# A graph kernel of hops, attention, messages and convolutions on one core: edge features stored by the counting and loaded per step, more PSUM banks per step, and fixed codes compared per edge

## The reference, cut to what matters

```python
for _ in range(10): out = spmm(out) * 0.9 + h * 0.1          # appnp hops over the degree-normed edges
...
m = relu(feat[src]) + EPS; a = softmax of m over the edges of each dst; msg = segment_sum(a * m, dst)
...
edge_feat = _mlp(edge_attr, W_edge, ...)                     # relu(attr @ W + b), normed over all edges
message = concatenate([x[row], x[col], edge_feat], axis=1)   # row, col = src, dst
msg = _mlp(message, W_msg, ...)                              # relu, then mean and variance over all edges
out = segment_sum(msg, col)
```

## Time and profile before

| what | value |
|---|---|
| median of 3 runs | 2815.78 us (2812.81 to 2824.91) |
| the profiled execution | 2801.42 us, span 2799.7 us |
| busy, share of the span | PE 1853.1 us (66%), PEld 1446.8 (52%), DVE 1564.5 (56%), POOL 936.1 (33%), ACT 861.7 (31%) |
| granted TensorE clock, mean | 0.735 |
| counting, 50 to 604 us | 554 us |
| message stage, 1404 to 2621 us | 1217 us, 43% of the span |

### The profile page before, as it was taken

The page is one execution under the profiler, slowest core; times in us unless marked ns, Lnnn a source line. Parts: engine busy times, 40 slices in busy tenths (PEclk is TensorE's granted clock), DMA queues, the critical chain, the costliest instruction groups (busy, mean ns, idle before and its releaser), DMA issues. The chain is left out here.

```text
span 2799.7 us, 50246 instructions
## 1 busy us (share of the span) xinstructions
PE 1853.1 (66%) x14611; PEld 1446.8 (52%) x14611; DVE 1564.5 (56%) x4031; ACT 861.7 (31%) x1484; POOL 936.1 (33%) x1182
## 2 busy tenths in 40 slices
PE   1777777779999999778525544544555555555488
PEld 0333444459999999745413433333444344333477
DVE  7856866665444444465434555555555555555753
ACT  1687566641111111121212222222222222222420
POOL 3311211131000000000166666666666666666100
PEclk9988988879999999889755555555555555555699
DMA  4211111110000000800132222222222222222200
GB/s 138 93 49 41 42 70 56 70 63 2 2 2 2 2 2 2 311 1 3 37 44 49 49 49 48 47 49 48 50 50 49 49 50 49 49 48 48 69 1 18
DMA packets 86652, 133.19 MB, mean 48 GB/s; under 512 B 48616, under 2 KB 55656, under 8 KB 86462
## 3 DMA queue, kind: packets, MB, share of 16 engines
q1 hardware_dynamic: 40398, 83.53, 8.8%
q0 software_dynamic: 25344, 38.98, 6.9%
q10 hardware_dynamic: 20720, 8.06, 1.3%
HBM read 95.89 MB, written 34.58 MB: 47 GB/s over the span
## 5 line engine op out<-in xcount | busy, mean ns | idle before, releaser
L1430 POOL DMA_INDIRECT counts<-p_rows,rows x784 | 745.6, 951 | 498.4 <-issue 224.0
L931 PE MATMUL ps_hop<-y,counts 128*128 128x192 f16 x6250 | 525.0, 247 | 21.6 <-DVEq L818 12.3
L1659 PE MATMUL ps_e_z<-e_w_q,counts 128*128 128x96 f32 x1568 | 364.1, 427 | 259.8 <-ACT counts L1595 219.9
L931 PEld LDWEIGHTS ps_hop<-y,counts 128*128 128x128 f16 x6250 | 520.0, 98 | 26.5 <-DVEq L818 12.4
L1659 PEld LDWEIGHTS ps_e_z<-e_w_q,counts 128*128 128x128 f32 x1568 | 341.8, 330 | 295.8 <-ACT counts L1595 249.9
L560 DVE TENSOR_TENSOR hot_w<-iota_w,places_now 128x1600 f16<-128x1600 f16 x300 | 297.0, 990 | 156.0 <-PE ps_counts L586 137.1
L586 PE MATMUL ps_counts<-hot_w,hot_p 128*128 x1196 | 287.6, 372 | 117.5 <-DVE hot_p L560 77.4
L1670 PE MATMUL ps_e_seg<-counts 128*128 128x192 f16 x784 | 140.7, 359 | 301.9 <-DVE counts L1470 151.1
L1670 PEld LDWEIGHTS ps_e_seg<-counts 128*128 128x128 f16 x784 | 100.4, 138 | 385.3 <-issue 198.2
L1595 ACT ACTIVATE counts<-ps_e_u 96x1024 f32<-96x1024 f32 x98 | 99.9, 1019 | 642.0 <-remote 591.1
L527 POOL TENSOR_TENSOR places_now<-places,origins (+1 forms) x302 | 115.4, 383 | 428.0 <-DVE hot_p L560 278.3
(11 more groups left out here) (401 smaller groups left out, 2483.4 us busy)
## 6 DMA issues: line engine op xcount, KB each, us to landing
counts<-count_rows SPq DMA_DIRECT2D x30, 800.0 KB, 6.6
count_rows<-attr_split SPq DMA_DIRECT2D x25, 800.0 KB, 3.8
counts<-p_rows,rows POOLq DMA_INDIRECT x784
e_attr<-attr_parts SPq DMA_DIRECT2D x99, 72.0 KB
attr_parts<-attr_split SPq DMA_DIRECT2D x9, 784.0 KB, 15.9
attr<-attr_parts SPq DMA_DIRECT2D x50, 140.6 KB
e_dst_rows<-dst_row SPq DMA_DIRECT2D x99, 64.0 KB
e_w_q<-q_rows ACTq DMA_DIRECT2D x392, 12.0 KB
```

The costliest lines, as they stand in the source:

```text
L931: mm = pe.matmul(ps[:, r, 0:2 * D], k.counts[:, m, b, :], y[:, odd, b, :], start=b == 0, stop=b == NB - 1)
L1430: nc.gpsimd.indirect_dma_start(z[:, slot, j, :], None, k.p_rows, bass.IndirectOffsetOnAxis(rows, 0)) \
L1659: mm = pe.matmul(ps_z[:, two, j // (STEP_TILES // 2), at:at + D], u_hot[:, two, j * P:(j + 1) * P], w_q[:, fed, j // Q_TILES, :], start=Tr ...
```

## The change

It does three things. **First**, the counting stores `u`, the relu of each unit of 2000 edges (768 KB), to the new `u_rows`, and the message loop loads 1024 columns of it (384 KB) into `u_hot` in place of the attributes: `edges` and `edge_mlp` are gone there, and `u_hot` has three buffers. In the counting the squares go to PSUM, `rectified(n)` waits until unit n-1 is stored, PE's `edges(n)` waits for `u_summed` in place of `u_taken`, and EARLY is spread over 11 blocks. **Second**, the message loop has three pairs of `ps_z` banks (ZS) and two `ps_s` banks (SUMS), three buffers of one-hots (MSG_HOTS); the squares are reduced over the eight tiles each step and added to totals in SBUF; PE does `messages(s+2)` ahead of `sums(s)`, and DVE `add_sums(s-2)` and `turned_hot(s+3)`. **Third**, the counting has two fixed f16 codes for each edge and one iota of 3200, of which each window takes its part, so POOL's `places` are gone; DVE's batches are one loop per window, with table loads on DVE's sequencer, and `hot_p` comes ahead of `hot_w`; SP's program is written out for all 25 blocks.

```diff
+        k.u_rows = nc.dram_tensor("u_rows", (D, TILES * P), F32, kind="Internal").ap()
...
-            k.window_tabs = part.enter_context(nc.sbuf_tensor("window_tabs", [1, 1 + 2 * NW], I32))
-
-            k.places = part.enter_context(nc.sbuf_tensor("places", [P, TILES + BATCH, 2], F32))
+            k.window_tabs = part.enter_context(nc.sbuf_tensor("window_tabs", [1, NW], I32))
+
+            k.codes = part.enter_context(nc.sbuf_tensor("codes", [P, TILES + BATCH, 2, 2], F16))
+            k.iota_c = part.enter_context(nc.sbuf_tensor("iota_c", [P, CODES], F16))
...
+            step(nc.vector.tensor_scalar(dst_i[:, :], dst_i[:, :], NOWHERE - (P - 1), None, ALU.bitwise_and))
+            nc.vector.memset(k.codes[:, TILES:, :, :], NO_PLACE)
+            nc.vector.scalar_tensor_tensor(k.codes[:, 0:TILES, 1, :], twice(part_i[:, 0, :]), float(WIDE),
+                                           twice(part_f[:, :]), ALU.mult, ALU.add)
+            nc.vector.scalar_tensor_tensor(k.codes[:, 0:TILES, 0, :], twice(dst_i[:, :]), -float(FIRST), twice(src_i[:, :]),
+                                           ALU.add, ALU.add)
             dve.wait_ge(steps_in, 16)
             step(nc.vector.tensor_copy(step_f[0:STEPS, :], step_i[0:STEPS, :]))
...
-    EARLY = [7, 7, 6, 5, 5]
+    EARLY = [5, 4, 4, 4, 4, 3, 3, 3, 2, 2, 2]
...
+        halves = k.attr_split[:, :, :, :].rearrange("p a r e -> p (a r e)")
+        staged = halves.bitcast(F16)[:, 0:2 * NB * P].rearrange("p (a b s) -> p a b s", a=2, b=NB)
+        attr = halves[0:PRODUCTS + 3, 2 * NB * P:2 * NB * P + U_PARTS * U_EDGES]
...
+            def store(n):
+                sp.wait_ge(u_taken, n + 1)
+                sp.dma_start(k.u_rows[:, bass.ds(n * (U_PARTS * U_EDGES), U_PARTS * U_EDGES)],
+                             u[:, :, :].rearrange("p a e -> p (a e)")).then_inc(u_stored, 16)
+
             def one_block(d, odd):
                 for n, _ in units_of(d):
 
                     if not isinstance(n, int) or n:
                         sp.wait_ge(u_done, n)
                     load(n)
+                    if not isinstance(n, int) or n:
+                        store(n - 1)
 
...
             sp.wait_ge(k.parts_stored, 16 * 9)
+            sp.wait_ge(pad_set, 1)
+            sp.dma_start(k.u_rows[:, E:TILES * P], u[:, 0, 0:U_PAD]).then_inc(u_stored, 16)
             sp.wait_ge(ones_set, 1)
-            for_blocks(sp, one_block)
+            for d in range(NB):
+                one_block(d, d % 2)
+            store(U_UNITS - 1)
+            sp.wait_ge(u_stored, 16 * (U_UNITS + 1))
...
+            nc.gpsimd.memset(zeros[:, :], 0.0).then_inc(zeros_set, 1)
+            nc.gpsimd.memset(u[:, 0, 0:U_PAD], 0.0).then_inc(pad_set, 1)
+            pool.wait_ge(k.parts_stored, 16 * 9)
             nc.gpsimd.memset(attr[:, :], 1.0).then_inc(ones_set, 1)
...
-            def places(i, tile, w):
-
-                pool.wait_ge(hot_ready, i + 1)
-                nc.gpsimd.tensor_tensor(
-                    now[:, bass.ds(i & 3, 1), :, :, :].rearrange("p a j c t -> p (a j) c t"),
-                    k.places[:, bass.ds(tile, BATCH), :].unsqueeze(3).broadcast_to([P, BATCH, 2, 2]),
-                    origins[:, bass.ds(w, 1), :].unsqueeze(3).broadcast_to([P, BATCH, 2, 2]),
-                    ALU.subtract).then_inc(places_ready, 1)
...
-                for q in range(4):
-                    s = q % 2
-                    dve.wait_ge(places_ready, four * 4 + (q + 3))
-
-                    dve.wait_ge(hot_used, four * 4 + (q + 1))
-                    for hot, n, c in ((hot_w, WIDE, 1), (hot_p, P, 0)):
+            first = 0
+            for w in range(NW):
+                d, j = w // WINDOWS, w % WINDOWS
+                n, tile_of_first = window_of(dve, w)
+                end = dve.snap(first + n)
+                shift = dve.snap(first * BATCH - tile_of_first)
+                with dve.Fori(first, end) as i:
+                    tile = i * BATCH - shift
+
+                    dve.wait_ge(hot_used, i + 1)
+                    for hot, lo, n, c in ((hot_p, d * P, P, 0), (hot_w, j * WIDE, WIDE, 1)):
                         made = nc.vector.tensor_tensor(
-                            hot[:, s, :, :].rearrange("p j (e t) -> p j e t", t=2),
-                            iota_w[:, 0:n].rearrange("p (e t) -> p e t", t=2).unsqueeze(1)
+                            hot[:, bass.ds(i & (HOTS - 1), 1), :, :].rearrange("p a j (e t) -> p (a j) e t", t=2),
+                            k.iota_c[:, lo:lo + n].rearrange("p (e t) -> p e t", t=2).unsqueeze(1)
                             .broadcast_to([P, BATCH, n // 2, 2]),
-                            now[:, q, :, c, :].unsqueeze(2).broadcast_to([P, BATCH, n // 2, 2]), ALU.is_equal)
+                            k.codes[:, bass.ds(tile, BATCH), c, :].unsqueeze(2).broadcast_to([P, BATCH, n // 2, 2]),
+                            ALU.is_equal)
                     made.then_inc(hot_ready, 1)
+                first = end
...
-                    pe.wait_ge(u_taken, n)
+                    pe.wait_ge(u_summed, n)
...
+                act.wait_ge(u_stored, n * 16 + 16)
                 nc.scalar.activation(u[:, :, :], ps_u[:, :, 0:U_EDGES], ACT.Relu,
                                      accum_out=u_sums[:, 0, bass.ds(n, 1)]).then_inc(u_taken, 1)
 
             def squares(n):
                 act.wait_ge(u_taken, n + 1)
-                nc.scalar.activation(u[:, :, :], u[:, :, :], ACT.Square,
+                nc.scalar.activation(ps_u[:, :, 0:U_EDGES], u[:, :, :], ACT.Square,
                                      accum_out=u_sums[:, 1, bass.ds(n, 1)]).then_inc(u_summed, 1)
...
+    ZS = MSG_HOTS = 3
+    SUMS = 2
...
+        hot_end = z_end + MSG_HOTS * STEP_TILES * P // 2
+        u_end = hot_end + FED * STEP
...
-        ps_u = ctx.enter_context(nc.psum_tensor("ps_e_u", [D, 2, BANK], F32))
-        ps_z = ctx.enter_context(nc.psum_tensor("ps_e_z", [P, 2, 2, BANK], F32))
-        ps_s = ctx.enter_context(nc.psum_tensor("ps_e_seg", [P, BANK], F32))
-        ps_sq = ctx.enter_context(nc.psum_tensor("ps_e_sq", [P, BANK], F32))
-        sq_sum = ps_sq[:, 0:HALF_BANK]
-        ones_set, w_set = sem("ones_set"), sem("w_set")
+        ps_z = ctx.enter_context(nc.psum_tensor("ps_e_z", [P, ZS, 2, BANK], F32))
+        ps_s = ctx.enter_context(nc.psum_tensor("ps_e_seg", [P, SUMS, BANK], F32))
+        w_set = sem("w_set")
...
-                sp.dma_start(attr[0:PRODUCTS, fed, :], k.attr_parts[:, bass.ds(s * STEP, STEP)]).then_inc(landed, 16)
+                sp.dma_start(u_hot[0:D, fed, :], k.u_rows[:, bass.ds(s * STEP, STEP)]).then_inc(landed, 16)
...
-                if s >= 2:
-                    dve.wait_ge(z_done, s - 1)
+                if s >= FED:
+                    dve.wait_ge(z_done, s - FED + 1)
...
-            def hots(s, two, places):
-                if s >= 2:
-
-                    dve.wait_ge(seg_done, s - 1)
+            def hots(s, places):
+                if s >= MSG_HOTS:
+
+                    dve.wait_ge(seg_done, s - MSG_HOTS + 1)
...
+            def squares_of():
+                return z_sq[:, :, :].rearrange("p j f -> p f j")
...
-                dve.wait_ge(sq_added, s + 1)
-                nc.vector.tensor_tensor(sq_sum, sq_sum, halves(z_sq)[:, 0, :], ALU.add).then_inc(sq_half, 1)
-                dve.wait_ge(sq_half, s + 1)
-                nc.vector.tensor_tensor(sq_sum, sq_sum, halves(z_sq)[:, 1, :], ALU.add).then_inc(sq_added, 1)
-
...
+                if s:
+                    dve.wait_ge(sq_added, s)
+                nc.vector.tensor_reduce(sq_step[:, :], squares_of(), AX.X, ALU.add).then_inc(sq_taken, 1)
+                dve.wait_ge(sq_taken, s + 1)
+                nc.vector.tensor_tensor(k.totals[:, 1, :], k.totals[:, 1, :], sq_step[:, :], ALU.add).then_inc(sq_added, 1)
...
+            def low_half(s):
                 dve.wait_ge(z_relu, s + 1)
-                low_part(two).then_inc(z_low, 1)
-
-            def joined():
-                return ps_s[:, 0:2 * D].rearrange("p (a f) -> p f a", a=2)
+                low_part(s % 2, s % ZS).then_inc(z_low, 1)
...
+                nc.vector.tensor_reduce(step_sum[:, :], joined(s % SUMS), AX.X, ALU.add).then_inc(seg_joined, 1)
...
-            nc.vector.memset(attr[:, :, :], 1.0).then_inc(ones_set, 1)
...
-                add_rows(s, s % 2, s % SLOTS, s // SLOTS + 1)
-                if s:
-                    add_sums(s - 1)
+                add_rows(s, s % ZS, s % SLOTS, s // SLOTS + 1)
+                if s >= 2:
+                    add_sums(s - 2)
                 if s + 1 < STEPS:
-                    hots(s + 1, (s + 1) % 2, step_places(s + 1))
...
-                    turned_hot(s + 2, s % 2, (s + 2) % FED, (s + 2) // FED + 1, step_nodes(s + 2))
+                if s + FED < STEPS:
+                    turned_hot(s + FED, s % FED, s // FED + 2, step_nodes(s + FED))
...
-            def edge_mlp(s, two):
-                act.wait_ge(u_done, s + 1)
-
```

(33 more changed lines are left out.)

229 lines of the change are left out of this document (84 added, 145 removed).

## The result

The changed kernel takes **3019.16 us** (median of 4 runs, 3017.47 to 3021.91) against 2814.3 us before (4 runs, 2811.28 to 2824.91): ratio 1.0722, 95% interval 1.0692 to 1.0751. The forecast was 2754, faster. Its profiled execution has a span of 3017.7 us against 2799.7, so 218.0 us are to be explained, some 13 more than the medians are apart, since the profiled execution before was a fast one.

| stage, us | before | after | difference | forecast |
|---|---|---|---|---|
| counting, with setup | 604.0 | 780.8 | +176.8 | +5 |
| ten hops | 582.0 | 597.5 | +15.5 | 0 |
| attention, preparation | 221.1 | 216.7 | -4.4 | -2.6 |
| message stage | 1214.0 | 1244.1 | +30.1 | -64 |
| the rest | 178.6 | 178.5 | 0 | 0 |

The account below looks back on a forecast made before the run. No engine was full; the message loop was taken as bound by POOL's gather bursts, with PE's signals held during them. Terms -64 - 2.6 + 5 = -61.6 us from 2801.4 gave 2739.8, plus 14.4 to the median 2754; range 2615 to 2830.

Parts of the forecast that it names:

- The load fits: 0.: Counting, late windows: DVE's table load, 0.287 us, fits into 0.42 us free per window, so it costs nothing.
- rival E: Counting: DVE's register work per window lies in series with its compares, +94 us, 2848 in all; chance 0.13.
- Nine units leave, nine enter: 0.: Counting: nine units leave the first five blocks, nine enter the six after, at 2.16 us a unit; net 0.
- ACT has slack there: 0: Counting, late blocks: a unit's store queued behind the counts' lands at 377.5, `rectified` stands at 377.04; cost 0.
- The +-20 for VectorE's part: Counting: bound put around the 0 forecast for the whole of DVE's part, +-20 us.
- PE's signals are held while POOL issues gathers: Message loop: bursts end when POOL runs out of freed slots; 16 gathers per burst, 12.01 us a step.
- three z banks, bursts of 24: Message loop: z of three steps stands ready, so bursts grow to 24 gathers, 11.34 us a step, -64 us.
- 24 x 1.249 + 4.04: Message loop: burst of 24 gathers plus pause, 34.0 us for three steps, 11.34 a step.
- The reduce, taken at 0.95 us: Message loop, DVE: reduce of 768 elements replacing adds, taken at 0.95 us; DVE +0.1 us a step, effect 0.
- Rival C: Message loop: signals are no longer held, POOL's 9.99 us a step sets the pace, -192, 2626; chance 0.18.
- rival D: Message loop: pace stays 12.01, by matmuls really ending late or bursts stopping after two steps; 2818; chance 0.12.
- the fill of `e_attr`: Ahead of the message loop's first feed: this fill of 2.62 us goes, -2.6 us.

Follow-up runs that it names:

- experiment 5: Changed kernel storing only 8 columns of each unit, message loop loading the same 1024 columns each step: 2729.68 us, beside a kernel before at 2595.8.
- experiment 2: Changed kernel with before's counting program (table bounded), keeping the stores, spread units and new message loop: 2909.28 us, ratio 1.0328 to the kernel before.
- experiment 6: Before's counting program, stores and new message loop, with `turned_hot(s+2)` right behind `add_rows(s)` in place of `turned_hot(s+3)` at the step's end: 2870.44 us, ratio 1.020.
- experiment 10: Later runs: experiment 6 with two pairs of z banks in place of three, 2682.56 us, ratio 1.033; changed kernel, unchanged, 2793.51 us, ratio 1.0762.

## Why the prediction was wrong

**The counting, +5 forecast, +177 measured.** It divides into spreading (31.5 in the traces, of which 17.7 is the units' and the rest late blocks at the lower clock), stores (48 by experiment 5) and codes (the other 97; 84 to 101 by experiment 2, of which VectorE's sequencer 73.5). Each part rests on single traces and is good to some 10 us. Five steps failed:

- *"The load fits: 0."* The load's own size was right (0.310 us median), and 0.42 us was free. But I counted one instruction where the whole sequencer's share stands in series, and the timeline has 0.67 us a window. It also falls on every batch: in the early blocks `hot_p` starts at 98.03 and 99.72, at 103.35 and 105.04, 1.69 us apart, where before the pair took 1.25 to 1.32. I had named it in rival E and priced it by POOL's worst load for late windows alone; E's +94 came near the codes' 84 to 101 by luck: 11 to 28 of them have nothing to do with VectorE's sequencer, and the early blocks have their part.
- *"Nine units leave, nine enter: 0."* I took the price of a unit (2.16 us) from a block with many batches, and used it where there are few: 5 to 9 us, part of it by the lower clock.
- *The stores, "ACT has slack there: 0".* I asked when a store lands, not what it slows. A store of 800 KB and one of 750 start within 1.1 us at a block's start, and the table loads beside them take up to 1.67 us, just where PE waits for its first batch. With hardly any stores VectorE's 200 loads take 74.3 us in place of 113.8.
- *The clock* was not in the sum at all. The same work took 14.6 or 17.1 us a block by it, and it averaged 0.69 in the changed kernel's counting, and in stretches of 60 to 70 us of before's, up to 580 us, it stood at 0.80 to 1.00.
- The +-20 for VectorE's part rested on the first step, and so did a range that left E out. (The forecast's own range is also added wrongly: 2754 + 20 + 32 is 2806, not 2785.)

**The hops, 0 forecast, +15.5 measured,** in each of the five kernels traced with the new codes (594.5 to 597.5) and in none with the old. PE's matmuls cost the same (248 and 247 ns). The hops are a loop of five turns, and at each of its four turnings back PE stands idle for 4.3 to 4.8 us, where before it was 2.1 to 2.5; that is 9 of the 12.6 us by which the way from the first hop matmul to the last is longer (546.6 against 534.0). PE's group in 540 us of the hops, before and after:

```profile
L931 PE MATMUL ps_hop<-y,counts 128*128 128x192 f16 x6226 | 521.3, 247 | 9.2 <-DVE y L849 9.1
L918 PE MATMUL ps_hop<-y,counts 128*128 128x192 f16 x6190 | 522.4, 248 | 17.9 <-issue 12.6 <-DVE y L836 5.3
```

Around each turning the profile's instruction queue moves four packets in all five kernels with the new codes and three in the eleven others. So it looks like the loading of the loop's own instructions, which stand elsewhere in the longer or shorter program; no run tested it.

**The message loop, -64 forecast, +30 measured.** The reading "PE's signals are held while POOL issues gathers" held in the runs in which the change was timed first, and so did "three z banks, bursts of 24". What failed is the step *"24 x 1.249 + 4.04"*: I carried the pause over from bursts of 16. Longer bursts reach a stretch in which the instructions of PE, VectorE and ScalarE come late, so when signals pass VectorE has its own leftovers and `turned_hot` to do ahead of `add_rows`: 36.9 us for three steps. The order in VectorE's program is some 34 us of the stage, 17 to 40 by the scatter (experiment 6); without it the new loop gains 10 us on the trace before, a sixth of the 64, and pauses are still 5.8 us. That rest was not explained. The reduce, taken at 0.95 us, takes 1.446:

```profile
L1469 DVE TENSOR_REDUCE counts<-e_z_sq 128x96 f32<-128x768 f32 x94 | 135.9, 1446 | 7.9 <-issue 7.9
```

Where signals are held, it lies inside the gathers. The 384 KB feed was hidden, as forecast. Rival C, 9.99 us a step, is what happened in the later runs, but to both kernels (to the kernel before by its time alone), which no rival had: I held the pace for a matter of the program.

On end times, the Trainium skill ("Perfetto Trace Analysis", section "Tensor Engine Instruction (MATMUL, LD_WEIGHTS)") says that TensorE's are estimated. The traces show no end of a matmul by itself, but in experiment 10 the same matmuls, again 3.70 us a step, make `add_rows` wait 1.1 us in 96 steps, and in the burst above VectorE's own reduce, whose end is no estimate, signals late as well. So it was the signal and not the work that came late, and rival D's first cause falls.

**Right:** the bursts of 24, the place of the held signals, the fill of `e_attr` (-4.4 for -2.6), zero for POOL's subtractions.

## What to carry to other kernels

Work moved to an engine's sequencer is paid in series with that engine's instructions: count each load, register operation and loop of it per batch, not only the load, and look at what else uses the memory at that moment. A price per unit read in a block that is full hides its cover; read it where the unit will stand. And a pace set by waits that no instruction explains may not belong to the program: time the kernel on another chip and at another time before building on it. Before a difference between two programs is divided into parts, look how far traces of one program scatter: here up to 17 us in the counting and 23 us in the message stage.

## What the runs showed of the hardware

- In the earlier runs signals between engines, and VectorE's signal to itself, were held while GpSimd issued indirect gathers, in the burst shown until 1.7 to 3.8 us behind the last. In the later runs, on two other chips, nothing was held, and the same kernel before took 2595 in place of 2815 us.
- A table load on a sequencer has a median of 0.30 us and takes up to 1.67 us beside stores of 750 and 800 KB; 200 of them take 113.8 us, and 74.3 us with hardly any stores.
- The same 94 matmuls keep PE busy for 11.28 or 14.02 us by the granted clock (0.88 and 0.70).
- A loop of PE can cost 2.1 to 2.7 or 4.1 to 4.9 us of idle time at each turning back, by nothing but changes elsewhere in the program.
- A reduce over a strided axis, 768 elements to 96, takes 1.446 us, half as much again as a full-width operation of 0.951.
